# Routing four pairs ahead of the shared expert, with other statistics, slot and overflow steps, in a four-block kernel on one Trainium2 core

## The reference

```
x = x + tanh(g_xattn[0]) * attention(layernorm(x), ctx, ctx)
x = x + tanh(g_ffn[0])   * sparse_mlp(layernorm(x))            # top 102 of 1024
x = x + tanh(g_xattn[1]) * long_conv(ctx, ctx, layernorm(x))
x = x + tanh(g_ffn[1])   * moe(layernorm(x))                   # 64 experts, top 6, one shared
moe: scores = softmax(h @ gate.T); topk_w, topk_ids = top_k(scores, 6); topk_w /= sum(topk_w)
     routed = sum over the 6 experts of w * (silu(h g_e) * (h u_e)) d_e      # 176 wide
     shared = (silu(h g_s) * (h u_s)) d_s                                     # 352 wide
```

## Time and profile before

| | us |
|---|---|
| median of 3 runs | 983.22 (981.06 to 984.05) |
| profiled execution, its own time | 991.96 |
| its span | 990.3 |
| PE busy | 677.4 |
| DVE busy | 610.0 |
| POOL busy | 466.6 |
| ACT busy | 242.8 |

### The profile page before, as it was taken

The page is one execution under the profiler, slowest core; times in us unless marked ns, Lnnn a source line. Parts: engine busy times, 40 slices in busy tenths (PEclk is TensorE's granted clock), DMA queues, the critical chain, the costliest instruction groups (busy, mean ns, idle before and its releaser), DMA issues.

```text
span 990.3 us, 12738 instructions
## 1 busy us (share of the span) xinstructions
PE 677.4 (68%) x2938; PEld 523.5 (53%) x2938; DVE 610.0 (62%) x1804; ACT 242.8 (25%) x543; POOL 466.6 (47%) x499
## 2 busy tenths in 40 slices
PE   1389980000698777755666656499999999999941
PEld 1245540000676644433555544388888888888830
DVE  4777759999588769998565454344444444444414
ACT  1011217773132200001322231122222222222200
POOL 4377643630022200331566647256666666666643
PEclk9589995555799979985878887699999999999975
DMA  8145517850000135321222212279999999999875
GB/s 292 62 144 168 185 71 307 334 208 0 1 1 0 58 102 169 98 83 64 74 84 90 85 73 101 91 176 225 234 235 234 224 222 228 232 240 229 207 163 178
DMA packets 77483, 147.86 MB, mean 149 GB/s; under 512 B 10000, under 2 KB 48336, under 8 KB 77456
## 3 DMA queue, kind: packets, MB, share of 16 engines
q1 hardware_dynamic: 46272, 91.29, 27.8%
q0 software_dynamic: 30320, 55.35, 23.4%
q10 hardware_dynamic: 864, 0.93, 0.3%
HBM read 83.75 MB, written 63.78 MB: 149 GB/s over the span
## 4 chain that ended last, share of the span: by engine, by line
PE 46%; DVE 25%; issue 11%; DMA 6%; another core or an unknown queue 5%; DVEq 2%; POOL 1%; ACT 1%; SPq 1%; POOLq 0%; ACTq 0%
PE psum L890 10%; PE psum L707 6%; PE psum L903 5%; PE psum L905 5%; PE psum L894 5%; PE psum L878 3%; PE psum L747 3%; DVE qT L1255 2%; DMA acc<-hh,toki 2%; DVE hh L1298 2%; PE psum L689 1%; PE psum L679 1%; DVE Z L1405 1%; DVE hh L1354 1%
## 5 line engine op out<-in xcount | busy, mean ns | idle before, releaser
L638 POOL DMA_INDIRECT acc<-hh,toki x128 | 199.3, 1557 | 112.8 <-DVE hh L1624 78.5
L615 POOL DMA_INDIRECT xs_rows<-Z,slot x96 | 93.7, 976 | 72.5 <-DVE slot L1524 45.3
L890 PE MATMUL psum<-qT,Z 128*128 128x256 f32 x512 | 122.7, 383 | 0.0
L890 PEld LDWEIGHTS psum<-qT,Z 128*128 128x128 f32 x512 | 93.4, 192 | 10.6 <-issue 0.3
L536 POOL TENSOR_TENSOR rstd<-mv,neghalf 128x1 f32<-128x1 f32 (+1 forms) x48 | 30.5, 636 | 141.5 <-DVE mv L1125 141.5
L1624 DVE TENSOR_SCALAR hh<-psum,wtok 128x256 f32<-128x256 f32 x128 | 56.1, 480 | 66.0 <-PE psum L905 54.2
L903 PE MATMUL psum<-Z,qT 128*128 128x256 f32 x256 | 77.2, 384 | 2.9 <-DVE qT L1614 2.9
L1612 DVE TENSOR_TENSOR qT<-H,psum 128x256 f32<-128x256 f32 x64 | 27.0, 421 | 81.8 <-ACT H L1067 81.8
L905 PE MATMUL psum<-wt,qT 128*128 128x256 f32 x256 | 76.8, 382 | 0.0
L1061 ACT ACTIVATE qT<-psum 128x512 f32<-128x512 f32 x64 | 38.2, 597 | 141.3 <-PE psum L878 131.5
L707 PE MATMUL psum<-wt,hTs 128*128 128x512 f32 x128 | 63.8, 644 | 13.0 <-ACT hTs L971 8.4
(11 more groups left out here) (280 smaller groups left out, 1420.5 us busy)
## 6 DMA issues: line engine op xcount, KB each, us to landing
Z<-in_wexp SPq DMA_DIRECT2D x66, 496.0 KB
xs_rows<-fill POOLq DMA_DIRECT2D x64, 272.0 KB, 2.8
Z<-xs_rows SPq DMA_DIRECT2D x64, 272.0 KB
kv_rows<-Z SPq DMA_DIRECT2D x12, 688.0 KB, 3.9
Z<-kv_rows SPq DMA_DIRECT2D x12, 688.0 KB, 4.2
acc<-fill POOLq DMA_DIRECT2D x4, 1024.0 KB, 8.2
ctxH_s<-in_ctxH SPq DMA_DIRECT2D x16, 224.0 KB, 3.9
wt<-in_wd SPq DMA_DIRECT2D x66, 48.0 KB
```

Of the source, the lines that this page charges most:

```text
L615: pool.indirect_dma_start(out=xs_rows[:, :], out_offset=bass.IndirectOffsetOnAxis(ap=slot[:, 2 * u + q, k:k + 1], axis=0), in_=H[:, 2 * u ...
L638: pool.indirect_dma_start(out=acc[s % 2][:, :], out_offset=bass.IndirectOffsetOnAxis(ap=toki[:, g, j:j + 1], axis=0), in_=y_sb[:, s, j, :] ...
L890: m = pe.matmul(pA[par][:, g * CAP:(g + 1) * CAP], wgu_sb[:, s, k, g * P:(g + 1) * P], xT[:, par, k, :], start=(k == 0), stop=(k == 1))
```

## The change

1. The statistics of the third block's result are taken in groups of four tiles, after the group's four additions (`x3`). PE's turns go in four groups, with `logits(0)` after the second and `logits(1)` after the third. The pairs 0 and 1 are normalised after eight tiles, and the last group of four is done after `choose(0)`.
2. `normalise` writes `H` alone, and PE turns from `H`. The turned pairs have eight places (`xTs`), no longer two.
3. `choose` sets the six largest logits to -3e38 by two MATCH_REPLACE and makes the mask by a comparison; the one-hot is gone. `place` multiplies rank + base + 1 by the mask and takes the largest 8 of 64 by MAX8; expert bases rise with the expert's number, and the six values less one are the slots.
4. The shared expert of pair `u - 4` runs behind the routing of pair `u`. The shared expert of the pairs 4 to 7 comes after the overflow chain. Its output has one PSUM bank, no longer two. No hardware loop is left in this part.
5. Overflow blocks go in pairs (two places for rows, weights and results), in padding and at the end. `back[1]` is read by SP in four pieces before it waits for the overflow blocks.

```diff
+    LAG = 4
-                    rank_and_share(2 * i + par, par)
+            for u in range(NPAIR):
+                ranks(u, u % 2)
+                if u + 2 < NPAIR:
+                    logits(u + 2, u % 2)
+                if u >= LAG:
+                    shared(u - LAG, (u - LAG) % 2)
...
             m.then_inc(brow_done, 1)
+            for u in range(NPAIR - LAG, NPAIR):
+                shared(u, u % 2)
             pe.wait_ge(ov_ready, 1)
...
+                pe.wait_ge(shid_ready, 3 * u + 3)
+                if u:
+                    pe.wait_ge(base_ready, u)
...
+                link(dve.tensor_copy(top6[:, par, :, 0:K], top8[:, par, :, 0:K]))
+                dve.match_replace(lgr[:, par, 0, :], top6[:, par, 0, :], lg[:, par, 0, :], TAKEN)
+                link(dve.match_replace(lgr[:, par, 1, :], top6[:, par, 1, :], lg[:, par, 1, :], TAKEN))
+                dve.tensor_scalar(mask[:, par], lgr[:, par], TAKEN, None, ALU.is_equal).then_inc(mask_ready, 1)
-                for q in range(2):
-                    m = dve.tensor_tensor(oh[:, par, q], iota_e[...], idxf[...], ALU.is_equal)
-                dve.tensor_reduce(mask[:, par], oh[:, par]..., AX.X, ALU.max).then_inc(mask_ready, 1)
...
+                link(dve.tensor_tensor(posr[:, :, :], posr[:, :, :], mask[:, par], ALU.mult))
+                dve.max(slotf[:, 0, :], posr[:, 0, :])
+                link(dve.max(slotf[:, 1, :], posr[:, 1, :]))
-                    m = dve.tensor_tensor(prod[:, q], oh[:, par, q], posr[...], ALU.mult)
-                link(dve.tensor_reduce(slotf[:, :, :], prod[:, :, :, :], AX.X, ALU.add))
...
+            x3(0)
+            x3(1)
+            dve.wait_ge(c_done, 2)
+            normalise(0)
+            normalise(1)
+            x3(2)
+            for u in range(NPAIR):
+                choose(u, u % 2)
+                if u == 0:
+                    x3(3)
+                if u > LAG:
+                    shared_out(u - LAG - 1, (u - LAG - 1) % 2)
+                if u + 2 < NPAIR:
+                    normalise(u + 2)
+                place(u, u % 2)
+                if u >= LAG:
+                    shared_hidden(u - LAG, (u - LAG) % 2)
+            shared_out(NPAIR - LAG - 1, (NPAIR - LAG - 1) % 2)
...
+            for u in range(NPAIR - LAG, NPAIR):
+                shared_hidden(u, u % 2)
+                shared_out(u, u % 2)
...
+            sp.wait_ge(added[1], 32 * (E // 2))
+            for c in range(4):
+                sp.dma_start(back[1][:, 4 * c:4 * c + 4, :], acc[1][...]).then_inc(early_in[c], 16)
+            sp.wait_ge(o_yr, 2 * n + 1)
+            sp.wait_ge(o_add, 32 * n)
-            pool.dma_start(back[1][:, :, :], acc[1][0:T, :]...).then_inc(early_in, 16)
```

More of the change, by code:

```diff
@@ L336, in build @@
         sum_done = sem("sum_done")
-        sum3_step, early_in = sem("sum3_step"), sem("early_in")
+        sum3_step = sem("sum3_step")
+        early_in = [sem(f"early_in{c}") for c in range(4)]
         back_in = [sem(f"back_in{c}") for c in range(4)]
@@ L625, in _ @@
                 alone(pool, "pool")
-                pool.indirect_dma_start(out=xs_rows[:, :], out_offset=bass.IndirectOffsetOnAxis(ap=gcol[:, 0:1], axis=0),
-                                        in_=fill[:, 0, :], in_offset=None).then_inc(padded, 16)
+                for j in range(2):
+                    pool.indirect_dma_start(out=xs_rows[:, :], out_offset=bass.IndirectOffsetOnAxis(ap=gcol[:, j:j + 1], axis=0),
+                                            in_=fill[:, j, :], in_offset=None).then_inc(padded, 16)
+                    pool.wait_ge(padded, 32 * b + 16 * j + 16)
+                    alone(pool, "pool")
             def add_rows(i, g, first):
@@ new lines, in _ @@
+                for j in range(2):
+                    pe.wait_ge(o_x[j], 16 * b + 16)
+                    for k in range(2):
+                        m = pe.transpose(pT[j][:, k * P:(k + 1) * P], xs_sb[:, j, 0, k * P:(k + 1) * P], ident[:, :])
+                    m.then_inc(o_T, 1)
+                for j in range(2):
+                    pe.wait_ge(o_w[j], 32 * b + 32)
+                    pe.wait_ge(o_Tr, 2 * b + j + 1)
+                    for g in range(2):
+                        for k in range(2):
+                            pe.matmul(pA[j][:, g * P:(g + 1) * P], wgu_sb[:, j, k, g * P:(g + 1) * P],
+                                      xT[:, j, k, 0:P], start=(k == 0), stop=(k == 1))
+                    for k in range(2):
+                        m = pe.matmul(pC[j][0:GU - 2 * P, 0:P], wgu_sb[:, j, k, 2 * P:GU],
+                                      xT[:, j, k, 0:P], start=(k == 0), stop=(k == 1))
+                    m.then_inc(o_gu, 1)
@@ L950, in _ @@
+                for j in range(2):
+                    pe.wait_ge(o_hid, 2 * b + j + 1)
+                    pe.matmul(pY[j][:, 0:D], hid0[:, j, 0:P], wd0_sb[:, j, :], start=True, stop=False)
+                    pe.matmul(pY[j][:, 0:D], hid1[:, j, 0:P], wd1_sb[:, j, :], start=False, stop=True).then_inc(o_y, 1)
         @block.scalar
@@ L1666, in _ @@
-            dve.wait_ge(early_in, 16)
+                for j in range(2):
+                    dve.wait_ge(o_x[j], 16 * b + 16)
+                    dve.wait_ge(o_free, b + 1)
+                    alone(dve, "dve")
+                    dve.scalar_tensor_tensor(wsel[:, j, 0, :], xs_sb[:, j, 0, CE:CE + K], ovcol[:, j:j + 1],
+                                             xs_sb[:, j, 0, CW:CW + K], ALU.is_equal, ALU.mult, accum_out=wtok[:, j, 0:1])
+                    dve.tensor_copy(toki[:, j, 0:1], xs_sb[:, j, 0, CT:CT + 1]).then_inc(o_tok, 1)
```

286 lines of the change are left out of this document (121 added, 165 removed).

## The result

The changed kernel took 1002.23 us (998.47 to 1005.17) beside 983.54 us before: ratio 1.0198 (95% interval 1.0161 to 1.0235). The forecast was 960.2 with a range of 940 to 980, so it failed in sign. The span went from 990.3 to 999.6 us, in three parts: the experts start at 654.92 for 631.75 (+23.2), they take 5.9 us less, and the end takes 8.0 us less: +9.3.

The account below looks back on a forecast made before the run. Late signals beside POOL's scatters were taken to pace the routing, and DMAs to bound the end. Gains of 14.7 us before the experts and 8.3 at the end, 23.0 in all, gave 960.2 us, range 940 to 980.

Parts of the forecast that it names:

- The view of before: Routing, 472 to 626: no engine full; PE's signals seen 1.5 to 6.7 us late beside POOL's scatters set the pace.
- First scatter: Start of routing: an earlier first pair puts the first scatter at 470 for 472.7, bounds 466 and 473.
- Part 4: Routing and shared expert, run four pairs apart: experts start at 617 for 631.75, a gain of 14.7 us.
- s = 3: Routing: PE's signals are seen 3 us late beside scatters, from values of 3.5, 3.5 and 1.9.
- the sum: PE and DVE chain: ranks about 463, four pairs at 7.2 to 492, 561, overflow chain to 572 to 574, experts 617.
- four shared pairs: After the overflow chain, PE alone: two at 12 us reach 598, two at 9 reach 616.
- The experts: Expert stretch, 644 to 945: the change touches nothing there, so it only moves in time.
- The end: Kernel's end: `back[0]` read at 967 for 975.24, gain 8.3 us, bounds 0 and 9.
- the mark of failure: Kernel's end: `back[0]` read later than 12 us behind `back[1]` would show the forecast wrong.
- Longer lag, slower than before: Routing: every signal may take 6.7 us beside unpaused scatters; experts 16 us later, 8 us slower, 991; chance 0.12.
- No lag: Routing: signals near 0 us late, scatters bound, experts at 597; gain 35 + 8.3 = 43 us, 940; chance 0.13.
- Scatters stretch: Scatters: all 1.263 us for 0.960, ending at 620, experts at 626; gain 6 + 8.3, 969; chance 0.08.

Follow-up runs that it names:

- LAG 0: Changed kernel, but a pair's shared expert stands behind the same pair's ranks: 983.01 us (chip 2), 981.55 us (chip 13), ratios 0.9934 and 0.9917 to the kernel before.
- noticks: Changed kernel without the three DVE signals a pair for which nobody waits: 936.61 us, one run on chip 11, where the kernel before took 954.73.

## Why the prediction was wrong, step by step

- *The view of before.* Right: the pace is set by late signals beside scatters, not by a busy engine. Chips without lag run the kernel before 26.5 to 36 us faster; that this is the lag, too, is argued, since no trace shows that kernel there.
- *First scatter*: forecast 470, measured 466.5. Choose and place are shorter, but DVE was not what was late: with LAG 0 the experts start at 632.9 in spite of both, for 627.4 in the kernel before on the same chip (13).
- *The step that failed*: Part 4's "I take s = 3 ... since POOL will now never pause", a constant, and for PE's signals alone. That POOL never pauses was the reason to expect more. The value came from the last run of before, which has 24 scatters, and left aside the 6.7 us of the loop; the new run has 48. Measured beside it: 9.4 and 10.7 us for PE's signals, and 1 to 7 us for DVE's own, for which the sum had no term at all, since in before they came at once. Up to the ranks of pair 3 the sum held (485.0 for 484.6, which is 463 and three pairs of 7.2; the first ranks came 4 us early), since late signals began only some 10 us into the run. The next pair, to the ranks of pair 4, took 37.2 us for 7.2 (522.1 for 492). This one pair is 30 of the 39 us by which the overflow chain came late (599.6 for 561); the pairs 4 to 7 lost the other 9. There the last run of 24 has 9.2 us for PE's last signal, where the same length in before had 3.5.
- *After that the sums held*: overflow chain 16 us for 11 (of which 9.2 is that last signal), four shared pairs 39 for 43, at 9.0 each once POOL was done. Experts 654.9 for 617.
- *The experts*: forecast unchanged, measured 5.9 us shorter from first turn to last product, which before ended at 945.22:

```profile
944.63 0.59 PE L905 MATMUL psum<-wt,qT 128*128 128x256 f32 x2
```
  Before, PE stood mostly idle ahead of the experts (busy 2.9 of 16 us, granted clock 0.50, the level of 1.2 GHz). Now it comes from the shared pairs at a granted clock of 1.00 (2.4 GHz). So its first eight records take 1.97 us, not 3.51, and it waits 1.24 us for the first product, not 2.90. From the first turn to the start of the fourth group of four turns it takes 10.3 us for 15.5, which is 5.2 of the 5.9:

```profile
633.65 3.51 PE L890 MATMUL psum<-qT,Z 128*128 128x256 f32 x8
...
643.94 1.22 PE L903 MATMUL psum<-Z,qT 128*128 128x256 f32 x2 [2.90 <-DVE qT L1614]
```
- *The end*: forecast 8.3, measured 8.0, near by luck in part. `back[0]` came 13.3 us behind `back[1]` (19.8 before), beyond the 12 that I had set as the mark of failure, since the second addition starts only 8.4 us after the first, which has to land beside the read. This gap gives 6.5 of the 8.0; 0.6 lie ahead of `back[1]` and 0.9 behind `back[0]`, where the sum had nothing.
- *Rivals*: "Longer lag, slower than before" had the sign and the place, and 0.12 of the chance; its price was 16 us at the experts' start, measured 23.2. It too had one s for all signals (6.7) and no term for DVE's own. "No lag" (experts from 597) is what noticks shows on chip 11: 589.9, overflow chain at 531 for 535. "Scatters stretch" is out: the median is 0.963. That the lag might come from the loop's form, the argument of "no lag" for itself, is out too: no loop is left, and the lag is.
- *The rule on the semaphore's cost* (the Trainium skill, TensorE: Matmul & The Clock Gate, Part 3, The cost: per-tile semaphore tail, about 26 ns per increment) is about increments of packed tiles that queue behind one another, not about when another engine sees one. It settles nothing here: the rows show 0.04 us from PE's end to DVE without lag, and 10.7 us with it.

Open: what makes a chip lag, whether it stays with the chip, and by what path the issue or the completion of indirect DMAs holds up the signals of PE and DVE and not those of ACT. No run here looks inside.

## What to carry to other kernels

A delay that was read beside one length of burst must not be carried to a longer one: ask what the change does to the length of the burst, and whether the delay ends with the pause behind it. Look for waits of an engine for its own last operation; they say that signals, not work, are late. Before a gain of a few per cent is believed, run it on more than one chip, and prefer the order that is faster on both kinds.

## What was not expected of the hardware

- On lagging chips, beside 48 indirect DMAs in a row, 1.265 us apart, DVE waited up to 7.31 us for itself; beside 96, one signal of PE took 28.2 us. The first 10 us of the run show nothing. With pauses of 4 to 6.5 us after every 12 (LAG 0) DVE's waits for its own signals stay at 0.16 us or less; those for PE do not go away (4.5 to 5.7 us from the end of a pair's last product to DVE, in six of the eight pairs).
- ACT's signals are in time in the same runs: 0.04 us to DVE in the midst of the run of 96 (555.44 to 555.48), 0.05 us to PE in the run of 48.
- The lag depends neither on the bytes (less than half: 6.44 for 6.45 us) nor on the rows (half: 6.40), and four waits and seven signals of DVE fewer in a pair leave it.
- It is there on some chips and not on others: 1014.56 and 929.35 us for one program.
